# Three slots for raw weights instead of four, two for the second block instead of three, and eleven slots for x instead of ten

## The reference

```python
# layer 0; layer 1 has the same form, with its adapter's output doubled
result = jnp.einsum('bsd,od->bso', x, base_weight) + base_bias
h = jnp.einsum('bsd,brd->bsr', x, lora_A_w[adapter_ids])
result = result + jnp.einsum('bsr,bor->bso', h, lora_B_w[adapter_ids])
...
x = x + _L0_cond_ref(x, itok_B_6_15, ...)
x = x + _L1_cond_ref(x, itok_B_0_23, ...)
```

## Time and profile before

| | us |
|---|---|
| median of 3 runs (2212.15 to 2214.28) | 2214.27 |
| the profiled execution | 2214.27 |
| its span, first to last instruction | 2212.5 |
| TensorE busy | 2083.8 |
| VectorE busy | 1530.1 |
| ScalarE busy | 725.5 |
| GpSimd busy | 674.2 |
| DMA, mean of the 16 engines, 222 GB/s | 72.8% of the span |

### The profile page before, as it was taken

The page is one execution under the profiler, slowest core; times in us unless marked ns, Lnnn a source line. Parts: engine busy times, 40 slices in busy tenths (PEclk is TensorE's granted clock), DMA queues, the critical chain, the costliest instruction groups (busy, mean ns, idle before and its releaser), DMA issues.

```text
span 2212.5 us, 27248 instructions
## 1 busy us (share of the span) xinstructions
PE 2083.8 (94%) x9196; PEld 1709.8 (77%) x9196; DVE 1530.1 (69%) x2128; ACT 725.5 (33%) x1264; POOL 674.2 (30%) x490
## 2 busy tenths in 40 slices
PE   3856999999999999999999999999999999999999
PEld 3745788777878787888777888877888777888887
DVE  2424677864777875677866777866777875867875
ACT  4632222322223233333333333333333323333332
POOL 0002140444131445230444221444322344312343
PEclk8977999999999999999999999999999999999999
DMA  7999885799674789564689564689554679654676
GB/s 217 363 282 326 255 245 165 242 294 318 195 207 117 222 267 315 149 190 124 213 252 317 158 188 124 215 248 303 180 173 134 209 231 313 197 160 145 200 221 195
DMA packets 355895, 490.51 MB, mean 222 GB/s; under 512 B 28972, under 2 KB 153900, under 8 KB 355372
## 3 DMA queue, kind: packets, MB, share of 16 engines
q1 hardware_dynamic: 355756, 488.77, 72.8%
HBM read 411.06 MB, written 77.60 MB: 221 GB/s over the span
## 4 chain that ended last, share of the span: by engine, by line
PE 66%; DMA 13%; DVE 8%; SPq 5%; issue 2%; POOL 2%; ACT 1%; POOLq 0%; DVEq 0%; ACTq 0%
PE acc L1244 20%; PE acc L1246 20%; PE acc L1245 20%; DMA w_second<-v_t 6%; DMA w_second<-wc_t 4%; DVE w_lo L877 3%; POOL w_raw L714 2%; PE h_acc L1175 2%; PE h_acc L1179 2%; DVE x_sum L889 1%; DVE c_out L1004 1%; DMA b_raw<-pb_t 1%; DMA hb_t<-e_raw 1%; SPq L456 1%; SPq L476 1%
## 5 line engine op out<-in xcount | busy, mean ns | idle before, releaser
L714 POOL TENSOR_TENSOR w_raw<-w_raw,w_second 128x512 f32<-128x512 f32 x480 | 672.6, 1403 | 1524.0 <-DMA w_second<-wc_t 886.9
L1244 PE MATMUL acc<-xop_hi,w_hi 128*128 128x512 f32 x2688 | 1055.7, 393 | 50.0 <-DVE w_lo L877 45.5
L1245 PE MATMUL acc<-xop_hi,w_lo 128*128 128x512 f32 x2688 | 1049.8, 391 | 0.0
L1246 PE MATMUL acc<-xop_lo,w_hi 128*128 128x512 f32 x2688 | 1049.6, 390 | 0.0
L877 DVE TENSOR_TENSOR w_lo<-w_raw,w_hi 128x512 fp32r<-128x512 f32 x672 | 567.7, 847 | 479.7 <-ACT w_hi L760 475.2
L760 ACT ACTIVATE w_hi<-w_raw 128x512 fp32r<-128x512 f32 x672 | 423.6, 631 | 1224.4 <-PE acc L1246 898.7
L1244 PEld LDWEIGHTS acc<-xop_hi,w_hi 128*128 128x128 f32 x2688 | 506.9, 189 | 174.1 <-DVE w_lo L877 65.4
L1246 PEld LDWEIGHTS acc<-xop_lo,w_hi 128*128 128x128 f32 x2688 | 506.7, 189 | 106.5
L1245 PEld LDWEIGHTS acc<-xop_hi,w_lo 128*128 128x128 f32 x2688 | 506.9, 189 | 103.7
L1004 DVE TENSOR_TENSOR c_out<-acc,c_out 128x512 f32<-128x512 f32 x352 | 233.4, 681 | 7.9 <-PE acc L1189 6.2
L889 DVE TENSOR_TENSOR x_sum<-x_in 128x512 f32<-128x512 f32 x240 | 230.4, 971 | 0.0
(11 more groups left out here) (99 smaller groups left out, 698.8 us busy)
## 6 DMA issues: line engine op xcount, KB each, us to landing
w_raw<-wc_t SPq DMA_DIRECT2D x448, 256.0 KB, 3.8
w_second<-wc_t SPq DMA_DIRECT2D x320, 256.0 KB, 4.9
w_raw<-v_t SPq DMA_DIRECT2D x224, 256.0 KB, 4.3
w_second<-v_t SPq DMA_DIRECT2D x160, 256.0 KB, 5.2
x_in<-x_t SPq DMA_DIRECT2D x128, 256.0 KB, 6.7
out_t<-c_out SPq DMA_DIRECT2D x128, 256.0 KB, 5.3
w_in<-w_t SPq DMA_DIRECT2D x16, 1024.0 KB, 7.8
v_t<-v_raw SPq DMA_DIRECT2D x16, 1024.0 KB, 8.3
```

What stands on the lines that cost most here:

```text
L714: nc.gpsimd.tensor_tensor(w_raw[:, r, :], w_raw[:, r, :], w_second[:, n % RAW2, :], ALU.add if sign > 0 else ALU.subtract).then_inc(w_summ ...
L1244: nc.tensor.matmul(bank[:, :], wh, xh, start=(k == 0), stop=False)
L1245: nc.tensor.matmul(bank[:, :], wl, xh, start=False, stop=False)
L1246: mm = nc.tensor.matmul(bank[:, :], wh, xl, start=False, stop=end)
```

## The change

One slot less of `w_raw` and of `w_second`, which together free as many bytes as one slot more of `xop_hi` and `xop_lo` takes. SP loads weights five steps ahead instead of six. Tile 2 of the next product is split at step 8 instead of 14, tiles 3 and 4 at 14, 5 and 6 at 15 (the remainder of 6 at 16), 7 at 16; the sum of tile 5 is made at step 11 instead of 14. Two tiles of the first stage, which lie over the x ring, move by 2 KB.

```diff
--- before.py
+++ after.py
@@ -63,10 +63,10 @@
     QUADS = P // R2
     TT = T // P
     STEPS = MH * 2
-    RAW = 4
-    RAW2 = 3
+    RAW = 3
+    RAW2 = 2
     RING = 3
-    XRING = 10
+    XRING = 11
     XS = 3
     BANKS = 4
     assert KT == MT and MH == 8 and KH == 8 and BATCH * RANK == P and R2 == 32 and TT == 4
@@ -134,9 +134,9 @@
         return out
 
 
-    X_SUM_AT = (3, 5, 7, 9, 10, 14, 15, 15)
-    X_HI_AT = (4, 6, 14, 14, 15, 15, 16, 16)
-    X_LO_AT = (4, 6, 14, 14, 15, 15, 16, 16)
+    X_SUM_AT = (3, 5, 7, 9, 10, 11, 15, 15)
+    X_HI_AT = (4, 6, 8, 14, 14, 15, 15, 16)
+    X_LO_AT = (4, 6, 8, 14, 14, 15, 16, 16)
 
     def x_tiles_at(g, at):
 
@@ -257,8 +257,8 @@
         b0t_raw = over("b0t_raw", [P, KT, P], fp32, "x_in", 48 * K1)
         s_hi = over("s_hi", [P, KH, P], f32r, "xop_hi")
         s_lo = over("s_lo", [P, KH, P], f32r, "xop_lo")
-        v_hi = over("v_hi", [P, 2, 4, SW], f32r, "xop_hi", 4 * K1)
-        v_lo = over("v_lo", [P, 2, 4, SW], f32r, "xop_lo", 4 * K1)
+        v_hi = over("v_hi", [P, 2, 4, SW], f32r, "xop_hi", 6 * K1)
+        v_lo = over("v_lo", [P, 2, 4, SW], f32r, "xop_lo", 6 * K1)
 
         acc = [pb(f"acc{i}") for i in range(BANKS)]
         x_sum = [pb(f"x_sum{i}") for i in range(XS)]
@@ -610,7 +610,6 @@
                     load_w(0)
                     load_w(1)
                     load_w(2)
-                    load_w(3)
 
             for k in range(KH):
                 if k == 0:
@@ -631,10 +630,10 @@
             for g in range(NG):
                 q, j = divmod(g, STEPS)
                 pl, i = divmod(q, NPROD)
-                s = g + 6
+                s = g + 5
                 if g == 0:
+                    load_w(3)
                     load_w(4)
-                    load_w(5)
                 if s < NG:
                     load_w(s)
 
@@ -1071,12 +1070,12 @@
                 if j == 4 and i in (M4, M3) and PRE <= pl < NPL:
                     h_split_lo(pl, DOWN[i][0])
                 for qq, k in x_tiles_at(g, X_LO_AT):
-                    if k >= 2:
+                    if k >= 3:
                         x_split_lo(qq, k)
                 for qq, k in x_tiles_at(g, X_SUM_AT):
                     x_add(qq, k)
                 for qq, k in x_tiles_at(g, X_LO_AT):
-                    if k < 2:
+                    if k < 3:
                         x_split_lo(qq, k)
                 for b in b_units_at(g, B_SPLIT_AT):
                     b_split_lo(*b)
```

## The result

| | before | after |
|---|---|---|
| time, median | 2213.21 us (4 runs, 2208.30 to 2214.28) | 2281.90 us (4 runs, 2277.95 to 2291.16) |
| profiled execution, span | 2214.27, 2212.5 us | 2277.88, 2276.1 us |
| ratio after / before | | 1.031, 95% interval 1.0269 to 1.0351 |

The changed kernel is 3.1% slower, about 69 us. The sign was forecast, the size was not: 2219.5 us was the forecast and 2243 the end of the range.

The account below looks back on a forecast made before the run. TensorE, busy 94% of the span, was taken as the bound, so only its idle time counts. Terms 4.5 + 2 + 5 + 3 - 7.9 - 1.5 = +5.1 us on 2214.3 gave about 2219.5 us, range 2204 to 2243.

Parts of the forecast that it names:

- (1): SP's load stream: weights go out one turn later with one slot less; costs 4.5, 2 and 5 us in M7 and M6.
- a lead of 3.8: Up to 3.8 us that w_lo is ahead of its step, subtracted from 103.0 us for M7 and M6.
- M7 and M6, passes 2 to 4: Two-slot w_second loop of 3.22 us a step gives 99.2 us, level with 99.1; 1.5 us a pass added for DVE waits.
- Pass 0 and 1: M7 and M6: pass 0 bound by bytes, weights behind more loads, +2 us; pass 1 between loop and no loss, +5.
- Quiet stretches at nothing: M2 and M1: two w_second slots allow 2.77 us a step against 2.72, hidden by w_lo's lead, so no cost.
- Latency near 5 us: w_second's median landing in M7 and M6 of pass 2 falls from 6.8 to near 5 us with less queue.
- Start, +3: First product: three weight pairs loaded ahead instead of four, so the fourth comes late; 3 us, between 1.6 and 3.8.
- The x ring, -7.9 and -1.5: Less VectorE work ahead of w_lo saves 7.9 us in M1 of passes 0 to 4, 1.5 at other product changes.
- B: Rival, chance 0.14: second slot becomes the bound in summed steps with other traffic, 44 us less 7.9, 2250 us.
- Its own sign: What would show rival B: M2 and M1 lose time in every pass.
- A: Rival, chance 0.24: weights stay covered in M7 and M6, the x ring wins, 2206 us.
- C: Rival, chance 0.12: stalls only change place at product changes, start paid from slack in M3, 2214 us.

Follow-up runs that it names:

- e2: Kernel before with weights issued five steps ahead, three pairs loaded at the start, and w_raw cut from four slots to three: 2274.53 us, ratio 1.0257.
- e4: Kernel before with all slots kept, weights issued five steps ahead instead of six, three pairs loaded at the start instead of four: 2202.44 us, ratio 0.9938.
- e3: Kernel before with weights issued five steps ahead, three pairs loaded at the start, and w_second cut from three slots to two: 2243.29 us, ratio 1.0127.
- e10: Same kernel as e4, run again beside the kernel before: 2204.42 us, ratio 0.9958.
- e7: Kernel before, loading 8 instead of 512 columns of each x block in passes 2 to 5: 2192.43 us, ratio 0.9885.
- e5: Changed kernel with GpSimd's sum over half of the columns of each summed weight tile: 2207.47 us, ratio 0.9959.
- e12: Weight part of the change alone on the kernel before, x ring at ten slots, GpSimd's sum over half of the columns: 2213.93 us, ratio 0.9990.

## Why the prediction was wrong

**The step that failed** is the one on slots, in (1): "with one slot less they need the same two events. So no load moves against its turn's waits", and then a price from w_second's loop alone, "(5.0 + 1.43) / 2 = 3.22 a step". The events are indeed the same, but they come later, because each slot must make its round in fewer steps. Of the two rings only w_second's was reckoned. The one that w_raw makes, which holds w_hi, w_lo and SP's issue too, is 10.0 us over three slots, 3.33 a step, and never appears. By e2 against e4, losing one of its slots costs 72.1 us by itself, while the ring that was reckoned costs 40.9 (e3); nothing in the sum stood for the first.

For M7 and M6 of pass 2 the working can be closed. It gave 103.0 less a lead of 3.8, 99.2 us, and 107.7 was measured. 32 steps of 3.33 instead of 3.22 are 3.5 us. The lead of 3.8 wasn't there either: M1 ahead of it runs at 3.04 a step in w_raw's loop against a pace of 2.72, and w_lo's mean lead in M1 of passes 2 to 5 is 1.27 us, 2.5 less. These two are 6.0 of the 8.5; the rest I can't assign.

- **M7 and M6, passes 2 to 4**: forecast +4.5 in all, measured 8.6, 5.8 and 11.5, together +25.9. The forecast took the stretch before (99.1) as already lost to the same loop, so that the new loop would only replace the old. e4 shows that it was so in part at most: with the same slots it takes 93.4, and 95.9 in e10, and e7, without x's bytes, takes 92.7. So 3 to 6 of the old 9 us went with the order alone, and the loss from slots came on top.
- **Pass 0 and 1**: forecast +2 and +5, measured +8.7 and +10.7. I took pass 0 as bound by bytes at a DMA share of 0.98. But 6.5 of the 8.7 us are lost in its M7 alone, which goes from 44.5 to 51.0 us at 264 and 262 GB/s, while the M6 behind it moves 305 GB/s in both kernels. So M7's loss isn't the bytes'; e4 has 44.5 there.
- **Quiet stretches at nothing**: wrong in pass 5 (+4.9), where the latency is only 4.35 us on average, w_raw's round trip 8.94 us, and thus a step 2.98 against a pace of 2.82. The quiet 2.77 of the working was too low as well: w_second's own loop is 4.35 + 1.46 + 0.23 us there, 3.02 a step. In M1 of passes 2 to 5, w_raw's round trip is 9.12 us, 3.04 a step against 2.72; 16 steps use up most of the lead there, and the stall comes in M7.
- **Latency near 5 us**: right (5.2).
- **Start, +3**: measured +5.8 in the first product (75.6), but for another reason. I charged the pair loaded later. e4 loads it later too and takes 70.9; e2 and e3, with one slot less, take 75.4 and 75.2. Nearly all of it is the slots. (The 20.9 us that I called lost in this product before aren't all a wait: its row has TensorE busy 54.9 us at a granted clock of 0.85, where the full clock's pace would give 48.9.)
- **The x ring, -7.9 and -1.5**: the x_sum is gone from those steps, but M1 of passes 0 to 4 isn't at 43.5 to 44: it takes 46.8, 46.2, 44.9, 46.0 and 44.9. In passes 2 to 4 the old stall at the product's beginning is gone and a new one of about 1 us stands at its seventh step, from weights. Behind weights in time (e5) M1 does take 43.5 in passes 1 to 5. But e4, with ten slots and a full sum, has 43.8, 43.6 and 44.4 in passes 2 to 4, where it was 45.2, 44.8 and 45.4, and e12, with ten slots and the half sum, has 43.5 in each of these three. So most of the stall there that I put down to x_sum goes without the x ring as well. Its worth over the whole kernel, 6.5 us in e12 against e5, is near my 9.4, but only 1.9 of it are in M1 (263.5 to 261.6 in all six).
- **Rivals**: B named the place, "every summed step with x, c, output or B traffic", and a decision from 4.2 us of latency on, but priced 44 us for w_second only. That loop alone cost 40.9 us in e3, and the latency of pass 5, 4.35, is just beyond its point. What B lacked is the other ring. Its own sign, a loss in M2 and M1 of every pass, didn't show: M2 of passes 2 to 5 takes 47.1 us in both kernels, and M1 lost 1.4 us over all six passes. A (weights stay covered) is refuted by pass 5. C is refuted by the size.

What stays open: the x ring with eleven slots beside four and three weight slots wasn't tried; it takes 4 KB more of each partition than either kernel. How much of the half sum's gain is VectorE's is not separated. How much of the gain from the new order is B's, and how much that of x and output blocks, is open too.

Of the versions that do the whole work, the fastest is e4: all slots as before, weights issued five steps ahead, 2202.44 and 2204.42 us, 0.4 to 0.6% faster than before.

## What to carry to other kernels

Before a buffer loses a slot, write down its whole round trip, from the issue of its load through every operation until the last reader frees it and back to the issuing queue, and divide by the slots: it must be under the step's pace with some room, for each ring by itself, in the quiet stretches too. A ring that a producer waits for 1000 us is not therefore too large: look at what waits inside the loop (here w_hi, 0.9 us of 12.6), since that slack and what a shorter queue gives back (here 1.7 us of landing) is what there is to give up. In a queue that issues in order, try moving loads that block for a slot behind those that don't; here that alone was worth half a per cent, and one turn more lost it again.

## What the runs showed of the hardware

- A w_lo takes 0.68 us in the earlier trace rows and 1.79 in the chain above, from 1190.34 on. GpSimd's next sum begins at 1190.3, by the tile's row, and lasts 1.26 us. The Trainium skill, page SBUF — State Buffer, section Who interferes with whom, says that such a pair blocks one another; the trace agrees here. What the earlier trace rows showed for x_sum thus stands in the weights' own round trip now and then, 1.1 us of 10 in this turn, but it is rare in these stretches (6 of 96).
- The landing got shorter by less than the round trip had to. One w_raw slot and one w_second slot less took it from 6.63 to 4.91 us, 1.7 us of a round trip of 12.6, while the round trip had to fall by a quarter, 3.1 us, to stay even. The sum, w_hi and w_lo went from 3.7 to 3.2 us only, and the wait of SP before w_second grew by 0.7.
- Cutting x loads to 8 of their 512 columns (e7) was worth 1.15% to the kernel before, nearly all of it in M7 and M6: in passes 2 to 4 they take 92.7, 90.9 and 90.7 us where they took 99.1, 99.8 and 98.8.
